# Cosine stage: extra pieces of head steps with a query unit go into the projection's PSUM bank

## The reference, cut to what matters

```python
x = x + attn_a(layernorm(x))        # latent attention
x = x + ffn(layernorm(x))           # feed-forward "f"
x = x + attn_b(layernorm(x))        # cosine attention: the stage of this change
x = x + ffn(layernorm(x))           # feed-forward "g"
x = x + gated_linear_attention(layernorm(x))   # the recurrent block
...
def attn_b(x):
    xn = layernorm(x) * g_norm
    q = (xn @ Wq) as 16 heads of 128;  k, v = split(xn @ Wkv)   # one k and v for all heads
    q, k = l2norm(q * 16) * 4, l2norm(k) * 4
    out = softmax(q @ k.T) @ v
    return layernorm(out @ Wout) * g_out
def ffn(x):
    out = (x @ weight) * scale
    ...  # tanh of the row's norm, then a bound on it
```

## Time and profile before

| | us |
|---|---|
| median of 3 runs | 2155.48 |
| lowest and highest of them | 2153.45, 2155.86 |
| profiled execution, its own time | 2144.99 |
| its span, first to last instruction | 2143.1 |
| PE busy | 1944.1 (91%) |
| DVE busy | 1019.9 (48%) |
| ACT busy | 809.6 (38%) |
| mean granted PE clock | 0.981 |

### The profile page before, as it was taken

The page is one execution under the profiler, slowest core; times in us unless marked ns, Lnnn a source line. Parts: engine busy times, 40 slices in busy tenths (PEclk is TensorE's granted clock), DMA queues, the critical chain, the costliest instruction groups (busy, mean ns, idle before and its releaser), DMA issues. The chain is left out here.

```text
span 2143.1 us, 30267 instructions
## 1 busy us (share of the span) xinstructions
PE 1944.1 (91%) x11630; PEld 1242.0 (58%) x11630; DVE 1019.9 (48%) x2232; ACT 809.6 (38%) x1780; POOL 519.7 (24%) x621
## 2 busy tenths in 40 slices
PE   6999999999899999999999999978977799999875
PEld 4556666566566766676667666733344544545643
DVE  4555555545223233333333422259885565546453
ACT  2544535435233223332332333215424234445332
POOL 1322223223011010101010111025552143542221
PEclk9999999999999999999999999989989999999997
DMA  5000000000100000000000000020000000000001
GB/s 229 1 1 1 1 1 1 1 1 1 56 20 1 1 1 1 1 1 1 1 1 1 1 1 1 1 71 0 1 1 1 1 1 1 1 1 2 2 1 40
DMA packets 9773, 24.03 MB, mean 11 GB/s; under 512 B 2448, under 2 KB 6304, under 8 KB 8864
## 3 DMA queue, kind: packets, MB, share of 16 engines
q1 hardware_dynamic: 8336, 18.92, 2.4%
q10 hardware_dynamic: 1296, 3.18, 0.4%
HBM read 20.00 MB, written 2.10 MB: 10 GB/s over the span
## 5 line engine op out<-in xcount | busy, mean ns | idle before, releaser
L1489 PEld LDWEIGHTS cos_ps<-cos_vx,cos_probs 128*128 128x128 f32 x2048 | 238.7, 191 | 33.6 <-issue 28.7
L1489 PE MATMUL cos_ps<-cos_vx,cos_probs 128*128 128x129 f32 x2048 | 239.8, 275 | 4.2 <-DVE cos_on L1171 4.2
L1480 PE MATMUL cos_ps<-lead_room,cos_kT 128*128 128x512 f32 x512 | 232.6, 599 | 6.8 <-PEq L50 6.1
L1362 ACT ACTIVATE cos_probs<-cos_ps 128x512 f32<-128x512 f32 x256 | 150.9, 598 | 172.7 <-PE cos_ps L1480 171.7
L671 ACT ACTIVATE probs<-sc,nmax 128x512 f32<-128x512 f32 (+3 forms) x256 | 132.5, 525 | 167.0 <-DVE nmax L525 165.0
L1273 POOL TENSOR_TENSOR cos_qrs<-cos_qse,neg_half 128x4 f32<-128x4 f32 x59 | 59.4, 1006 | 507.1 <-DVE cos_qse L1153 507.1
L780 PE MATMUL sc<-kT,qT 128*128 128x512 f32 (+3 forms) x512 | 170.6, 455 | 3.9 <-DVE probsT L537 2.5
L1480 PEld LDWEIGHTS cos_ps<-lead_room,cos_kT 128*128 128x128 f32 x512 | 95.3, 192 | 107.2 <-issue 105.1
L2959 DVE TENSOR_REDUCE cos_wq<-tail_ps 128x2 f32<-128x1024 f32 (+3 forms) x128 | 101.7, 823 | 78.0 <-PE tail_ps L3199 76.9
L1151 DVE TENSOR_REDUCE cos_qss<-cos_qsq 128x4 f32<-128x512 f32 x59 | 40.5, 686 | 200.2 <-ACT cos_qsq L1341 200.2
L752 PE MATMUL pq<-xnT,wap 128*128 128x512 f32 x256 | 125.1, 612 | 4.1 <-DVE swp L517 4.1
(11 more groups left out here) (495 smaller groups left out, 3413.6 us busy)
## 6 DMA issues: line engine op xcount, KB each, us to landing
onT<-in_mla_wqT SPq DMA_DIRECT2D x1, 2048.0 KB, 9.6
lead_room<-in_mla_wo SPq DMA_DIRECT2D x1, 2048.0 KB, 19.9
cos_wq<-in_cos_wq SPq DMA_DIRECT2D x1, 2048.0 KB, 25.8
cos_wout<-in_cos_wout SPq DMA_DIRECT2D x1, 2048.0 KB, 7.5
out<-x SPq DMA_DIRECT2D x4, 512.0 KB, 2.9
x<-in_x SPq DMA_DIRECT2D x1, 1536.0 KB, 15.1
wq_pe<-in_mla_wq_pe ACTq DMA_DIRECT2D x1, 1024.0 KB, 14.6
x<-in_x SPq DMA_DIRECT2D x1, 512.0 KB, 4.3
```

The source lines that it names most:

```text
L1362: act.activation(probs[:, n % 2, kj, :], ps[:, kj, :], ACT.Exp).then_inc(s["e_done"], 1)
L1480: pe.matmul(ps[:, kj, :], kT[:, b % 2, kj * P:(kj + 1) * P], qT[:, hq % 2, h % 4, :], start=True, stop=True).then_inc(s["s_ready"], 1)
L1489: last = pe.matmul(po[:, qi // 2, qi % 2, :], probs[:, n % 2, kj, qi * P:(qi + 1) * P], vx[:, b % 2, kj, :], start=(kj == 0), stop=(kj == ...
```

## The change

A piece in a head step that has a unit is booked in bank 6 in place of bank 7; a piece in a step without one stays in bank 7. Everything else that differs (the waits of pieces, turns and projections) `cos_plan` works out from that.

```diff
@@ cos_plan
             if u is not None:
                 piece(("turn", "q", b, u))
             for key in cos_misc(b, h):
-                piece(key)
+                piece(key, 7 if u is None else 6)
         take(("outputs", b), (4, 5), ("y_done", "y_done"))
```

## The result

| | before | after |
|---|---|---|
| median, us | 2155.67 | 2131.73 |
| lowest of the runs | 2153.45 | 2127.38 |
| number of runs | 4 | 4 |
| profiled execution, its own time | 2144.99 | 2129.9 |
| its span | 2143.1 | 2128.0 |

The changed kernel takes 0.9891 of the time of the one before (95% interval 0.9871 to 0.991), 23.9 us less by the medians. One of the four runs of the kernel before took 4006.82 us; the median counts it, the ratio does not, and without it that median is 2155.48. The forecast was 2133.5 us, with a range of 2127 to 2142.

The account below looks back on a forecast made before the run. TensorE, busy 1944.1 of 2143.1 us, was taken as the bound. Gains of 22 x 0.85 and 7 x 0.50 us, less 0.2, made 22.0 us off the median of 2155.48: 2133.5 us, range 2127 to 2142.

Parts of the forecast that it names:

- The wait that goes: At 29 pieces in the cosine stage, TensorE's wait for ScalarE's copy of the turned queries vanishes; piece 0.46 us behind turn.
- Its size: Each removed wait of a piece was put at 1.31 - 0.46 = 0.85 us of TensorE's time; 22 pieces gain it whole.
- The seven with waiting scores: In 7 steps before a new group of four heads, scores wait for the turn's copy instead: 0.50 us gained each, 3.5 together.
- The projection's wait: The next projection into bank 6 must await the piece's reading; covered except in step 8 of batch 2, costing 0.2 us once.
- The turns: Turns wait for qn from their own projection, whose chain moves along; ScalarE's 1.12 us idle covers it: cost nothing.
- The second rival: ScalarE becomes late in the cosine stage: a 0.60 us copy reaches the turn at 16 pieces, 9.6 us lost, 2143.1; chance 0.08.
- The sum: Over the cosine stage, 18.7 + 3.5 = 22.2 us gained, less 0.2 for the projection's bank: 22.0 us.
- The sign that every other stage would stay as long: In the profile after, the cosine stage would be 22 us shorter and all other stages as long as before.
- ScalarE late: ScalarE's back-to-back copies of turn and piece delay its square and the next turn: 9.6 us lost, 2143.1 us; chance 0.08.
- The clock giving back more: Short idle times in the cosine stage had lowered TensorE's clock; closing them wins 3.9 us more, 2129.6 us; chance 0.03.
- The wait not being the bank's: Pieces wait for their own input, not bank 7, so nothing changes: 2155.5 us; chance 0.04.
- The slower one: Projections wait for bank 6 in all 29 steps, since pieces are read late: at 1.1 us each, 2165.2 us; chance 0.03.

Follow-up runs that it names:

- e3: Against the changed kernel, turned queries of steps with a unit go into bank 6 and the pieces stay in bank 7: 2127.17 us, ratio 0.9872 to the kernel before.
- e7: Changed kernel with six more VectorE reads of the bank ahead of each of six feed-forward products in steps 4 and 5: 2138.05 us, one run.
- e8: Kernel before, pieces still in bank 7, with six more VectorE reads ahead of each of six feed-forward products in steps 4 and 5: 2150.76 us, one run.
- e5: Changed kernel with one more 512-column ScalarE copy between the turn's copy and the piece in each of the 29 steps: 2127.62 us, one run.
- e6: Changed kernel with four more 512-column ScalarE copies between the turn's copy and the piece in each of the 29 steps: 2135.49 us, one run.
- e10: The changed kernel run again, unaltered, beside the kernel before on the same chip: 2127.98 us against 2151.12, ratio 0.9896.
- e1: Against the changed kernel, only the 22 pieces whose next scores do not wait use bank 6, the other 7 bank 7: 2133.23 us, ratio 0.991 to kernel before.
- e2: Against the changed kernel, only the 7 pieces whose next scores wait use bank 6, the other 22 bank 7: 2147.36 us, ratio 0.998 to kernel before.
- e4: Changed kernel, with output-phase projections and turns alternating between banks 6 and 7 and the next projection issued ahead of the turn: 2112.58 us, ratio 0.9812 to kernel before.

## Why the prediction was right

- **The wait that goes.** Right in mechanism and number: 29 waits of pieces, all gone, the piece 0.47 us behind its turn (forecast 0.46).
- **Its size.** 0.85 us was a little low: steps with rows gained 0.90, with products 0.95. I had taken the distance from turn to piece alone. A piece that comes out of a wait also needs longer up to the next instruction, 0.05 us for rows and 0.10 for products, and the rows already showed it: four matmuls of 128x128 took 0.50 us up to the next instruction behind a wait, and 0.46 without one. By steps: 7 with rows at 0.90 and 11 with products at 0.95, 0.66 in step 8 of batch 2, 0.75, 0.95 and 0.76 for the recurrent block's z1, q and z, make 19.9 for the 22.
- **The seven with waiting scores.** Right that they gain less, and where. Mis-sized: 0.39 and not 0.50, since the scores now come out of a wait and pay the 0.10 us themselves. 2.7 in place of 3.5.
- **The projection's wait.** Right in place (step 8 of batch 2 alone delays a matmul); it costs 0.30 instead of 0.2: the matmul is 0.20 us late, as forecast, and its own first 0.10 longer was not counted. e3 removes it, e7 and e8 show what it costs when the reading is later.
- **The turns.** Costed at nothing, and nothing was added: 22 waits of 12.7 us for qn before and after. e5 shows the room, e6 its end. The reason given was too simple, though: it read the cover of 1.12 us off one step and took it for all. Behind step 6 of batches 1 and 2 there was none before the change (a square right behind the exponents, shown at e5). These two got no later because ScalarE's own work moved with the change: behind the turn, the piece's copy and the squares after it come 0.86 us sooner, while the projection comes only 0.39 sooner. The second rival did allow for such fuller steps.
- **The sum.** 22.6 us by steps, forecast 22.0. The 22 whole steps, without the projection's wait, gained 20.2 and not 18.7, the seven 2.7 and not 3.5, and the wait took 0.3 and not 0.2. These errors are of opposite sign, so the sum fits better than its terms, which is partly luck. The absolute figure is luck in part as well: taking the gain off the median and not off the profiled execution was what made the forecast fit: 2144.99 less the gain would have given 2123.0, under the range, and the profiled execution after took 2129.9. The sign that every other stage would stay as long failed, by 7.3 us; e10 puts that down to the execution.
- **The rivals.** ScalarE late: refuted by e5 for the margin at hand. The clock giving back more: the granted clock was 1.00 in the stage in both profiles (0.50, that is 1.2 GHz, in its first 5 to 6 us, ahead of any piece, and 1.00 from there to the end), and the gain splits into steps without a rest. The Trainium skill, "TensorE: Matmul & The Clock Gate", section "A second HAM failure mode: psum-queue depth-cycling", describes a kernel in which small idle times between groups of matmuls make the clock swing. This trace shows no such swing at idle times of 0.69 us, before or after. The wait not being the bank's: refuted by e1 and e2, piece by piece. The slower one: the mechanism exists (e7), its condition does not. But its margin was put too wide: the worst reading ends 3.58 us behind the scores' start (1088.70 to 1092.28) and not 2.6, since the scores start sooner by what the piece gains and that reading does not.

## What to carry to other kernels

Where one engine fills a buffer twice in a row and another empties it, look for a second buffer that is already free at that moment: here the one whose reader must have finished before the first of the two fillings could start. Then check who fills that second buffer next, and how long after its last reading: the distance between the two (here 2.5 us for most steps, none for one) is what makes it free of charge. Cost a wait by the whole length of the step with and without it, not by its idle time alone, and compare executions stretch by stretch before a difference of spans is read as the change's.

## What was not expected of the hardware

- A wait of PE costs more than its idle time. The idle time shown was 0.69 us, the distance from turn to piece was 0.84 longer with it, the step 0.90 to 0.95; in e4, 0.59 us of idle time were worth 0.78. Of the 0.84, 0.16 is the overlap of two matmuls that a wait between them takes away. The first matmul behind a wait is shown 0.06 to 0.10 us longer, and its weight load starts with it (both at 1092.33 in step 8 of batch 2), where in step 6 of batch 1 the projection's load starts 0.42 us ahead of it, beside the matmul before (865.79 and 866.21). That the late load makes the matmul longer was not tested.
- In e6, after 2.18 us of waiting ahead of a turn, PE's granted clock fell for a few us, and 3.43 us of matmuls took 5.13; the same happened in batch 2. In e7 the longest wait was 2.19 us, ahead of a projection and behind scores, and the four matmuls of that projection took 1.98 us, their usual time behind a wait. So the length of the wait alone does not decide it; what does was not tested.
